# A graph layer on one core: who scales the first supers, how the first gathers get their indices, and where the short rest goes

## What is computed

```python
x_i = x[dst]; x_j = x[src]                                # x: 100000 x 48, f32
tmp = jnp.concatenate([x_i, x_j, edge_attr], axis=1)      # 25000 edges, 48 + 48 + 32 = 128 columns
h = jax.nn.relu(tmp @ W1 + b1)                            # 128 x 128
msg = h @ W2 + b2                                         # 128 x 48
out = jax.ops.segment_sum(msg, dst, num_segments=100000)
x = layernorm(x + out)                                    # over the 48 columns of each node
```

## Time and profile before

| | |
|---|---|
| median of three runs | 395.75 us (394.97 to 395.84) |
| profiled execution | 395.34 us, span 393.6 us, 18011 instructions |
| granted TensorE clock, mean | 0.989 |
| PE / DVE busy | 358.6 us (91%) / 369.7 us (94%) |
| ACT / POOL busy | 285.1 us (72%) / 281.6 us (72%) |
| DMA | 165601 packets, 66.38 MB, mean 169 GB/s |
| gathers on POOL (L877) | 196, 212.5 us, 1084 ns each |
| scalings on POOL (L886) | 72, 66.2 us, 920 ns each |

### The profile page before, as it was taken

One profiled execution on the slowest core, in us unless ns is written; L12 is line 12 of the kernel. 1 busy time (PEld: TensorE's weight loads), 2 busy tenths in 40 slices (PEclk: granted clock), 3 DMA queues, 4 the chain that ended last, 5 costly groups with the idle time before them and its releaser, 6 DMA issues.

```text
span 393.6 us, 18011 instructions
## 1 busy us (share of the span) xinstructions
PE 358.6 (91%) x6802; PEld 324.1 (82%) x6802; DVE 369.7 (94%) x1044; ACT 285.1 (72%) x791; POOL 281.6 (72%) x284
## 2 busy tenths in 40 slices
PE   3169999989999999999999999999999999999981
PEld 2047888878999999999998989998999999999971
DVE  6655999999999999999999999999999999999975
ACT  1046776776788787888787878878788878788861
POOL 6777777771688888888888888888888888212120
PEclk9999999999999999999999999999999999999995
DMA  4576889888878989989989989988988888753122
GB/s 87 103 152 129 134 182 212 182 180 206 181 160 178 185 180 183 198 181 201 206 166 231 200 173 198 218 186 177 231 181 176 199 191 164 174 152 98 49 81 78
DMA packets 165601, 66.38 MB, mean 169 GB/s; under 512 B 95213, under 2 KB 165554, under 8 KB 165554
## 3 DMA queue, kind: packets, MB, share of 16 engines
q1 hardware_dynamic: 152762, 58.74, 65.2%
q0 software_dynamic: 6272, 4.83, 9.7%
q10 hardware_dynamic: 6520, 2.26, 2.5%
HBM read 38.46 MB, written 27.33 MB: 167 GB/s over the span
## 4 chain that ended last, share of the span: by engine, by line
PE 66%; DVE 20%; POOL 4%; issue 4%; DMA 3%; ACTq 0%; SPq 0%; ACT 0%; DVEq 0%
PE bank L993 12%; PE bank L1013 11%; PE bank L1001 10%; PE bank L982 10%; PE bank L956 8%; PE bank L1020 8%; PE bank L950 6%; POOL rows L877 4%; DVE onehot L1262 3%; DVE sq_total L1280 3%; DVE ys L1238 3%; DVE total L1229 3%; DVE x_rest L1268 2%; DVE ys L1298 2%; DVE msg_rest L1245 1%
## 5 line engine op out<-in xcount | busy, mean ns | idle before, releaser
L877 POOL DMA_INDIRECT rows<-in_x_dram,src_cols x196 | 212.5, 1084 | 53.2 <-issue 50.4
L1082 ACT ACTIVATE onehot_t<-bank 128x384 bf16<-128x384 bf16 (+1 forms) x261 | 117.9, 491 | 18.4 <-PE bank L956 18.3
L1020 PEld LDWEIGHTS bank<-w,hid_t 128*128 128x128 f32 x522 | 95.5, 190 | 23.1
L886 POOL TENSOR_TENSOR ys<-ys,rstd 128x432 f32<-128x432 f32 x72 | 66.2, 920 | 46.3 <-DVE rstd L1288 45.2
L1020 PE MATMUL bank<-w,hid_t 128*128 128x48 f32 x522 | 82.5, 239 | 0.0
L956 PE MATMUL bank<-ident_b,onehot 128*128 128x128 bf16 (+1 forms) x782 | 73.1, 221 | 8.9 <-DVE onehot L1262 8.5
L1262 DVE TENSOR_SCALAR onehot<-node_of,cat 128x384 bf16<-128x384 f16 x260 | 69.0, 320 | 10.0 <-DMA cat<-edge_table 10.0
L1001 PE MATMUL bank<-cat_t,w 128*128 128x384 f32 (+1 forms) x176 | 71.3, 486 | 0.5 <-ACT cat_t L1070 0.5
L993 PE MATMUL bank<-msg,onehot 128*128 128x48 bf16 (+1 forms) x782 | 69.1, 184 | 2.2 <-DVE msg_low L1252 2.2
L1013 PEld LDWEIGHTS bank<-xs,onehot_t 128*128 128x128 bf16 (+1 forms) x782 | 69.2, 104 | 1.6 <-issue 0.9
L1013 PE MATMUL bank<-xs,onehot_t 128*128 128x48 bf16 (+1 forms) x782 | 69.6, 184 | 0.7 <-ACT onehot_t L1082 0.7
(11 more groups left out here) (109 smaller groups left out, 816.8 us busy)
## 6 DMA issues: line engine op xcount, KB each, us to landing
out_dram<-ys SPq DMA_DIRECT2D x43, 432.0 KB
xs<-in_x_dram SPq DMA_DIRECT2D x78, 216.0 KB
cat<-edge_table SPq DMA_DIRECT2D x261, 40.5 KB
edge_table<-rows SPq DMA_DIRECT2D x65, 121.5 KB
rows<-in_x_dram,src_cols POOLq DMA_INDIRECT x196
rows<-in_edge_attr_dram SPq DMA_DIRECT2D x28, 96.0 KB
xs<-in_x_dram ACTq DMA_DIRECT2D x8, 216.0 KB
rows<-in_edge_attr_dram ACTq DMA_DIRECT2D x1, 384.0 KB, 5.5
```

The lines of the kernel that those rows point to most:

```text
L877: pool.indirect_dma_start(rows[:, t, 0:D], None, x[:, :], bass.IndirectOffsetOnAxis(ap=src_cols[:, t:t + 1], axis=0)).then_inc(xsrc_in[s], 16)
L886: pool.tensor_tensor(y, y, rstd[0:n, v, 0:m].unsqueeze(2).broadcast_to([n, m, D]), ALU.mult).then_inc(normed, 1)
L1020: last = pe.matmul(msg_ps[:, k * D:(k + 1) * D], hid_t[:, v % SMALL, k * P:(k + 1) * P], w2[:, :], start=False, stop=(k == blocks - 1))
L1082: act.activation(onehot_t[0:n, v % SMALL, k, 0:jj * P], onehot_ps[k % 2][0:n, 0:jj * P], ACT.Copy).then_inc(onehot_t_ready, 1)
```

## The change

Three things are changed.

1. `FIRST_SCALED` goes from 12 to 6: POOL also scales supers 6 to 11. POOL's loop now starts with super 0 and, for the supers that DVE scales, only gathers. `LEAD` goes from 14 to 12. Who waits for the scaling of super g (`wait_scaled`: SP's stores, DVE's `invert` eight supers later) waits for both counts where both engines have scaled up to g.
2. The indices of the first three tiles are loaded once more, by three transfers at the head of ACT's queue, straight as columns into `src_first` (128 partitions, one index each). The first three gathers read them and wait for `src_first_in` alone; the fourth waits for `src_placed`.
3. The 160 nodes over become the third block of super 86: 53 partitions with three nodes, and partition 53 with one. There are 87 supers, all of one shape in the compute stages; what the last block computes for other partitions is not stored. The last super is loaded (`x`) and stored (`out`) by three transfers each (`last_rows`): two full blocks, 53 rows of 576 bytes, and one of 192. The constants for the short shape go.

```diff
-LEAD = 14
+LEAD = 12
-FIRST_SCALED = 12
+FIRST_SCALED = 6
 LAST_SCALED = 4
+LAST_PARTS = 3
...
-    RJ = 2
-    RP = REST // RJ
+    REST_P = REST // J
+    REST_J = REST - REST_P * J
     FULL_SUPERS = FULL // SUPER
-    NS = FULL_SUPERS + 2
+    NS = NB // SUPER
...
         def shape_of(g):
 
-            if isinstance(g, int) and g == NS - 1:
-                return RP, 1, RJ
-            return BP, FULL % SUPER if isinstance(g, int) and g == NS - 2 else SUPER, J
+            return BP, SUPER, J
...
+        def scaled_by_dve(g):
+
+            return g < FIRST_SCALED or g >= NS - LAST_SCALED
+
         def wait_scaled(eng, g):
 
-            if FIRST_SCALED <= g < NS - LAST_SCALED:
-                eng.wait_ge(normed, g - FIRST_SCALED + 1)
-            else:
-                eng.wait_ge(dve_normed, g + 1 if g < FIRST_SCALED else g + 1 - (NS - LAST_SCALED - FIRST_SCALED))
+            by_dve = sum(scaled_by_dve(k) for k in range(g + 1))
+            if by_dve:
+                eng.wait_ge(dve_normed, by_dve)
+            if g + 1 > by_dve:
+                eng.wait_ge(normed, g + 1 - by_dve)
...
+        def last_rows(table, tile):
+
+            w, first, s = J * D, FULL * BLOCK, (NS - 1) % BODY
+            before, here = (SUPER - 1) * w, (NS - 1) * SUPER
+            return ((table[0:first, :].rearrange("(b p j) d -> p b (j d)", p=BP, j=J)[:, here:FULL, :],
+                     tile[:, s, 0:before].rearrange("p (b m) -> p b m", b=SUPER - 1)),
+                    (table[first:first + REST_P * J, :].rearrange("(p j) d -> p (j d)", j=J),
+                     tile[0:REST_P, s, before:before + w]),
+                    (table[first + REST_P * J:N, :].rearrange("(p j) d -> p (j d)", j=REST_J),
+                     tile[REST_P:REST_P + 1, s, before:before + REST_J * D]))
...
             def store(g):
 
-                v, last = g % BODY, g >= NS - PAIR
-                if g % PAIR and not last:
-                    return
-                supers = 1 if last else PAIR
-                wait_scaled(sp, g + supers - 1)
-                sp.dma_start(dram_rows(out, g, supers), sbuf_rows(ys, g, v, supers)).then_inc(y_out[v // PAIR], 16)
+                v = g % BODY
+                if g == NS - 1:
+                    wait_scaled(sp, g)
+                    for there, here in last_rows(out, ys):
+                        sp.dma_start(there, here).then_inc(y_out[v // PAIR], 16)
+                elif g % PAIR == 0:
+                    wait_scaled(sp, g + PAIR - 1)
+                    sp.dma_start(dram_rows(out, g, PAIR), sbuf_rows(ys, v, PAIR)).then_inc(y_out[v // PAIR], 16)
...
-            pool.iota(short_node_i[:, :], pattern=[[1, RJ], [RJ, RP]], base=0, channel_multiplier=0).then_inc(consts, 1)
...
+                if t == GROUP:
+                    pool.wait_ge(src_placed, 1)
+                cols = src_first if t < GROUP else src_cols
                 pool.indirect_dma_start(rows[:, t, 0:D], None, x[:, :], bass.IndirectOffsetOnAxis(
-                    ap=src_cols[:, t:t + 1], axis=0)).then_inc(xsrc_in[s], 16)
+                    ap=cols[:, t:t + 1], axis=0)).then_inc(xsrc_in[s], 16)
...
-            pool.wait_ge(src_placed, 1)
+            pool.wait_ge(src_first_in, 16 * GROUP)
             gathered = 0
             needed = None
-            for g in range(FIRST_SCALED, NS):
+            for g in range(NS):
                 for gathered in range(gathered, tiles_for(g + LEAD)):
                     gather_xsrc(gathered)
                 gathered = tiles_for(g + LEAD)
...
-                if g < NS - LAST_SCALED:
+                if not scaled_by_dve(g):
                     scale(g)
...
+            for t in range(GROUP):
+                act.dma_start(src_first[:, t:t + 1], src[t * P:(t + 1) * P].rearrange("(p a) -> p a", a=1)).then_inc(src_first_in, 16)
             load_ends(act, 0, src, src_in)
...
             def less_high_x(g, r, v):
-                dve.wait_ge(x_in[v], 16 * (r + 1))
+                dve.wait_ge(x_in[v], 16 * (r + (LAST_PARTS if g == NS - 1 else 1)))
...
             def scale_some(g, r, v):
 
-                if FIRST_SCALED <= g < NS - LAST_SCALED:
+                if not scaled_by_dve(g):
                     return
```

More of the change, by code:

```diff
@@ L425, in gnn_resnorm_kernel @@
     EREST = E - EP * EC
-    assert NS % PAIR == 0 and BODY % PAIR == 0
+    assert NS % PAIR == 1 and BODY % PAIR == 0
     assert EP == P - 1 and 0 < EREST < EC
@@ L490, in gnn_resnorm_kernel @@
         src_cols = sb("src_cols", [P, EC], I32)
+        src_first = sb("src_first", [P, GROUP], I32)
         rows = sb("rows", [P, EC, ROW])
@@ L635, in shape_of @@
         def shape_of(g):
-            if isinstance(g, int) and g == NS - 1:
-                return RP, 1, RJ
-            return BP, FULL % SUPER if isinstance(g, int) and g == NS - 2 else SUPER, J
+            return BP, SUPER, J
         def first_block(g):
-            return FULL if isinstance(g, int) and g == NS - 1 else g * SUPER
+            return g * SUPER
         def walk(eng, stages, looped=True):
@@ L668, in walk, with sbuf_rows @@
                     run(stage, *divmod(t - k, BODY))
+        def scaled_by_dve(g):
+            return g < FIRST_SCALED or g >= NS - LAST_SCALED
         def wait_scaled(eng, g):
[L672 to L691 removed]
+            by_dve = sum(scaled_by_dve(k) for k in range(g + 1))
[3 more added lines that the diff above has]
+                eng.wait_ge(normed, g + 1 - by_dve)
+        def dram_rows(table, g, supers=1):
+            return table[0:FULL * BLOCK, :].rearrange("(b p j) d -> p b (j d)", p=BP, j=J)[:, g * SUPER:(g + supers) * SUPER, :]
+        def sbuf_rows(tile, s, supers=1):
+            return tile[:, s:s + supers, :].rearrange("p s (b m) -> p (s b) m", b=SUPER)
+        def last_rows(table, tile):
[7 more added lines that the diff above has]
+                     tile[REST_P:REST_P + 1, s, before:before + REST_J * D]))
         def rows_in(g, r):
@@ L812, in load_nodes @@
                     sp.wait_ge(sum_done, g - BODY + 1)
-                sp.dma_start(sbuf_rows(xs, g, v), dram_rows(x, g)).then_inc(x_in[v], 16)
-            def store(g):
-                v, last = g % BODY, g >= NS - PAIR
-                if g % PAIR and not last:
-                    return
-                supers = 1 if last else PAIR
-                wait_scaled(sp, g + supers - 1)
-                sp.dma_start(dram_rows(out, g, supers), sbuf_rows(ys, g, v, supers)).then_inc(y_out[v // PAIR], 16)
+                if g < NS - 1:
+                    sp.dma_start(sbuf_rows(xs, v), dram_rows(x, g)).then_inc(x_in[v], 16)
+                    return
+                for there, here in last_rows(x, xs):
+                    sp.dma_start(here, there).then_inc(x_in[v], 16)
+            def store(g):
+                v = g % BODY
[6 more added lines that the diff above has]
+                    sp.dma_start(dram_rows(out, g, PAIR), sbuf_rows(ys, v, PAIR)).then_inc(y_out[v // PAIR], 16)
             def nodes_behind(g):
@@ L843, in _ @@
                 pairs = len(range(s, NS // PAIR, BODY // PAIR))
-                sp.wait_ge(y_out[s], 16 * (pairs + 1 if s == (NS // PAIR - 1) % (BODY // PAIR) else pairs))
+                sp.wait_ge(y_out[s], 16 * (pairs + LAST_PARTS if s == (NS - 1) % BODY // PAIR else pairs))
             with sp.If(needed > 0):
@@ L906, in _ @@
             with pool.If(needed > 0):
-                pool.wait_ge(dve_normed, FIRST_SCALED + LAST_SCALED)
+                pool.wait_ge(dve_normed, sum(scaled_by_dve(g) for g in range(NS)))
                 general_engine["gpsimd"](pool)
@@ L1091, in copy_last_onehot @@
                 n, blocks, jj = shape_of(g)
-                if blocks == SUPER:
-                    copy_block(g, v, 2)
+                copy_block(g, v, 2)
             def relu(g, r, v):
@@ L1256, in make_onehot @@
                 n, blocks, jj = shape_of(g)
-                nodes = node_of if jj == J else short_node_of
                 dve.wait_ge(row_in[v], rows_in(g, r))
```

27 lines of the change are left out of this document (7 added, 20 removed).

## The result

The changed kernel takes 390.29 us (median of three runs, 389.61 to 390.47) against 395.75 before: ratio 0.9864, 95% interval 0.9846 to 0.9881. I had forecast 392.0 and a range of 390.4 to 394.3. The direction was right, and so was the largest term, the handover of the scaling. The profiled execution took 390.47 us with a span of 388.7, so by the two profiles the gain is 4.9.

The account below looks back on a forecast made before the run. It took DVE to bound the first supers and PE, with contention, the middle. Terms -3.31 + 0.10 - 0.75 + 0.4 = -3.56 took the profiled 395.34 us to 391.8, forecast as 392.0; range 390.4 to 394.3.

Parts of the forecast that it names:

- The bound and the pace: Per super: 4.545 us while DVE also scales, 3.994 in the middle at PE's pace with contention, 3.943 once gathers are over.
- Part 1: Scaling of supers 6 to 11 moved to POOL: 3.31 us saved, 0.10 lost to longer gathers, LEAD 12 at cost 0.
- the forecast 71 and 5: Handover sign: POOL's first scaling at about 71 us, behind a wait of some 5 us.
- Part 2: Start, with early source indices: 0.75 us gained; bounds a gain of 1.74 and a loss of 0.4.
- This wait goes. What is late next is PE: Start: DVE's 1.74 us idle for super 4's edge rows vanishes; PE then has only a 0.58 us gap to give.
- From here DVE is the bound: Start: from `total` of super 1 on, DVE sets the pace, so the start gives 0.75 us.
- Part 3: End, merged last super: 0.6 us gained, 1.0 lost to extra stores, net loss 0.4; bounds gain 1.0, loss 1.3.
- The slow last store: Rival, end: one engine moves the 53 rows, landing 2.2 us later than the single store: 393.2 us, chance 0.22.
- Better than forecast: Rival: no contention at the six moved supers and small stores hidden, another 0.3 + 1.0: 390.7 us, chance 0.10.
- POOL and DVE in each other's way at every super: Rival: each of six moved scalings lengthens a DVE operation by 0.53 us, leaving 0.5 of 3.31: 394.8 us, chance 0.10.
- SP as the bound: Rival, middle: edge-row landing and SP's delay together pass 10.7 us of slack; 1 us beyond gives 405 us, chance 0.04.
- The start giving nothing: Rival, start: small transfers land late or the late `dst` copy carries through, 0 or +0.4: 392.8 to 393.2, chance 0.12.

Follow-up runs that it names:

- The extra POOL work: Changed kernel plus one tiny POOL iota behind the scaling of each super from 20 to 59: ratio 1.0066 to the kernel before.
- the scaling part alone: Kernel before with only FIRST_SCALED 6 in place of 12 and LEAD 12 in place of 14: ratio 0.9927.
- the src columns alone: Kernel before with only the src_first loads on ACT's queue and the first gathers reading them: ratio 0.9945 (0.9926 to 0.9965).
- the repetition of the changed kernel: Changed kernel measured once more, unedited, against the kernel before: ratio 0.9876 (0.9847 to 0.9905).
- the cut into 48 and 5: Changed kernel with the last super's 53 rows moved as 48 and 5, for x loads and out stores: ratio 0.989 to the kernel before.
- the one with all three later edits: Changed kernel with POOL scaling from super 3, DVE scaling every eighth middle super, 53 rows as 48 and 5: 388.85 us, ratio 0.9837.
- taking work away from it: Changed kernel with DVE in place of POOL scaling every eighth super of the middle (9 to 65): ratio 0.9878 to the kernel before.
- a third with the split: Changed kernel with POOL scaling from super 3 and 53 rows moved as 48 and 5: 387.87 us, ratio 0.9812 to the kernel before.

## Why the prediction was right and wrong

**The bound and the pace, right, with a wrong reason.** The profile after has 4.54, 4.00 and 3.94 us a super for 4.545, 3.994 and 3.943, and the others have them too, apart from steps with a longer hold or an added edit. I took 3.994 for PE's pace with contention on top. The extra POOL work shows that POOL is just as full there, so the number was right to carry over and the picture behind it was not.

**Part 1, right to 0.3 us.** Forecast -3.31 + 0.10. Supers 2 to 14 show 53.82 - 50.34 = -3.5, or -3.4 with the scaling part alone. POOL's first scaling at 71.54 behind a wait of 6.32 us is the forecast 71 and 5. LEAD cost nothing. SP does wait longer for the gathers, as its largest wait after shows (such waits were 12.7 and 9.4 us before, 14 in all). In the profile after this reached nobody:

```profile
SPq L775 <- DMA rows<-in_x_dram,src_cols: 29.4, 19, 2.8
```

**Part 2, the step that failed.** "so the start gives 0.75 us" is the term that was mis-sized: it measured 1.0 in the first pair of profiles, 1.3 in the mean of all, and 2.2 (1.4 to 2.9) by the ratio of the src columns alone. What failed is what it was worked out from: "This wait goes. What is late next is PE". DVE's wait for the edge rows of super 4 was 1.50 to 1.74 us in the three profiles without the early columns. Of the eleven with them it is gone in three, the first among them, and 0.5 to 2.1 us long in eight. In the repetition of the changed kernel:

```profile
36.51 0.78 DVE L1276 TENSOR_SCALAR onehot<-node_of,cat 128x384 bf16<-128x384 f16 x3 [2.14 <-DMA cat<-edge_table]
```

What the early gathers did is to bring those one-hots 1.3 us forward, from a mean start of 37.12 to 35.82, and `total` of super 1 with them, from 41.58 to 40.34, whether DVE waited or not. So the price was the shift of the edge rows and not the length of one wait, and in single executions it is blurred: that `total` starts anywhere from 39.40 to 41.07 in the eleven. "From here DVE is the bound" held: from `total` of super 1 to `centre` of super 2 it is 5.49 to 5.69 us in all fourteen. Why the ratio shows more than super 2 does stays open. The first gather at 4.19 (3.9 forecast) and the copy of `dst` at 11.36 (11.1) were right.

**Part 3, near by luck.** Forecast +0.4, from two parts that were both too large and of opposite sign. The eight profiles with the merge and the 53 rows whole give 21.5 to 21.7 us from super 82 to the end, the three without the merge 21.4 to 21.5: +0.2. From super 82 to the end of the last scaling it gained 17.34 - 17.08 = 0.26 in place of 0.6; the stores cost 4.46 - 4.08 = 0.4 in place of 1.0.

**The miss of 1.7 us, added up.** In the two profiles that the sum spoke of, the start gave 1.0 in place of 0.75 (0.24 more), the handover and the middle 0.3 more, the end cost 0.1 in place of 0.4 (0.28 more), and before's profile held the one step of 4.84, 0.53 us that after's did not: 1.33, which is 391.8 against 390.47. The other 0.4 is in the medians, and is noise as far as any run shows. I added 0.2 for the profile of before lying 0.4 below its median, and the median of after came out 0.2 below its own profile. Why the first ratio, 5.4 us, is above the sum of the terms by the table, -3.4 - 1.3 + 0.2 = -4.5, stays open; the second measurement gave 4.9 +- 1.2, which holds it, and by the columns' own ratio the start is worth 0.9 more than the 1.3 in this sum.

**The rivals.** The slow last store was right in mechanism. I priced it at 2.2 us behind the single store of before where it measured 0.4, and the cut into 48 and 5 takes 0.3 to 0.5 back. Most of the slow transfer lies beside the large store and the third issue. "Better than forecast" came true in size, though not for its reasons: one of the six moved supers has a held `msg_rest` (0.82 us at 84.69), and the small stores were not hidden. POOL and DVE in each other's way at every super: no, one in four. SP as the bound: no sign in the profile after, where DVE's last wait for `cat` ends at 30.87. But one more kernel showed it, the one with all three later edits (waits of 1.53 and 1.04 us in the middle). The slack that the forecast put at 10.7 us is gone there at two supers. The start giving nothing: no.

**The range.** I had written down bounds of 1.74 for the gain of the start and 1.0 for that of the end. Together they make 392.0 - 1.0 - 1.4 = 389.6. The low end of 390.4 supposed that they would not meet, and left no room at all for the medians.

## What to carry to other kernels

Where a term of a forecast rests on the start of a kernel, take its spread from several executions before giving it two decimals; here the spread of the start was larger than the term. An engine that releases neither PE nor DVE in the middle can still set their pace by holding up operations that share a port with it: the test is to give it a tiny instruction more and see whether its price comes out in full. The reverse did not hold here: taking work away from it gave 0.1 to 0.4 us where 2.2 were forecast, since the next engines stood close behind. And a last store should have a number of rows that divides well; 48 and 5 ended 0.3 to 0.5 us earlier than 53 even with one more issue.

## What was not expected of the hardware

- The hold seems to go both ways. In the profile after, between 100 and 320 us, 40 of 123 gathers took 1.38 to 1.42 us, all of them beside `msg_low` and `x_low`; 70 took 0.94 to 0.97, nearly all beside `total`. But most of the 13 between, of 1.02 to 1.05, stood beside `x_rest`, `msg_low` and `x_low` as well, so which operation lengthens a gather is not shown.
- A hold can double: at one step a gather took 1.42 us in place of 1.05, and the hold of `msg_rest` behind it was 1.06 us (1.36 in all) in place of 0.53. That the first caused the second is read from the order of the rows, and no run tests it.
- The 27 matmuls of the last sum came at a granted clock of 1.00 in 0.85 us and at 0.50 (1.2 GHz) in 1.25. Two kernels with the split ran them at 0.50, a third with the split at 1.00. In two kernels without it, the repetition of the changed kernel among them, the clock fell inside the sum (0.78 in the mean, 0.96 us), where the first profile of that same code had 1.00. So the split is not needed for the fall. PE had been idle for 1.9 us before them each time. The lower level costs 0.4 us at the very end, where nothing hides it. Window of the sum in the repetition (columns as in the earlier trace rows):

```profile
380.43:381.39 0.96, 0.96 (x27) 0.83 (x27) 0.68 (x2) 0.00 (x0) 0.00 (x0) 0.78 0.00 0
```

- The profiles agree in the middle to some 0.02 us a step except for the held ones, while the time to reach super 2 differs by up to 1.5 us (45.04 to 46.57) between kernels whose code is the same up to there.
